# A three-layer interaction network on one core: the spread of the hidden half at its own relu, in two lays, and layer 1's weights on the x queue

## What is computed

```python
h = x0
for i in range(3):
    Wk = Ws[i].reshape(128, H, 32)            # H = 32, then 64, 64
    xk = relu(einsum('bhd,bmd,ohm->bod', h, x0, Wk) + b[i][None, :, None])
    if i != 2:
        outs.append(xk[:, :64]); h = xk[:, 64:]
    else:
        outs.append(xk)
return concatenate([o.sum(axis=-1) for o in outs], axis=1)      # (512, 256)
```

## Time and profile before

| | us |
|---|---|
| three runs | 1838.84, 1838.84, 1838.52 (median 1838.84) |
| the profiled execution, its own time | 1838.24 |
| its span | 1836.4 |
| PE busy | 1799.4 |
| DVE busy | 1555.1 |
| POOL busy | 1464.3 |
| ACT busy | 1096.3 |

### The profile page before, as it was taken

The page is one execution under the profiler, slowest core; times in us unless marked ns, Lnnn a source line. Parts: engine busy times, 40 slices in busy tenths (PEclk is TensorE's granted clock), DMA queues, the critical chain, the costliest instruction groups (busy, mean ns, idle before and its releaser), DMA issues.

```text
span 1836.4 us, 17679 instructions
## 1 busy us (share of the span) xinstructions
PE 1799.4 (98%) x6284; PEld 1184.2 (64%) x6284; DVE 1555.1 (85%) x851; ACT 1096.3 (60%) x899; POOL 1464.3 (80%) x323
## 2 busy tenths in 40 slices
PE   4899999999999999999999999999999999999998
PEld 2566666666666666666666666666666666666665
DVE  5989888888888888898888888888888988888886
ACT  3665666656566656656666565666566566665663
POOL 2787887877877878878878778778788788787785
PEclk9999999999999999999999999999999999999999
DMA  6333323323323333333233233233332332332310
GB/s 230 130 96 119 129 85 129 130 80 128 130 84 129 114 101 129 95 121 129 85 129 131 80 128 121 93 129 114 101 129 87 129 129 85 129 131 79 129 33 20
DMA packets 56455, 205.78 MB, mean 112 GB/s; under 512 B 12721, under 2 KB 14001, under 8 KB 47921
## 3 DMA queue, kind: packets, MB, share of 16 engines
q1 hardware_dynamic: 55408, 204.00, 33.3%
q10 hardware_dynamic: 960, 0.66, 0.1%
HBM read 153.75 MB, written 0.52 MB: 84 GB/s over the span
## 4 chain that ended last, share of the span: by engine, by line
PE 93%; issue 1%; DVE 1%; ACT 1%; POOL 0%; POOLq 0%; SPq 0%; DMA 0%; ACTq 0%
PE ACC L440 23%; PE ACC L456 19%; PE ACC L453 19%; PE ACC L450 19%; PE ACC L431 11%; PE ACC L434 3%; DVE ZS L257 1%; POOL ZL L339 0%; ACT ZH L361 0%; POOLq L71 0%; DVE ZW L252 0%; ACT HP L354 0%; DMA H<-H 0%; SPq L168 0%; DVE S L278 0%
## 5 line engine op out<-in xcount | busy, mean ns | idle before, releaser
L339 POOL TENSOR_TENSOR ZL<-ZS,ZH 128x2048 fp32r<-128x2048 f32 x319 | 1464.1, 4617 | 366.5 <-ACT ZH L361 366.5
L361 ACT ACTIVATE ZH<-ZS 128x2048 fp32r<-128x2048 f32 x384 | 734.6, 1913 | 599.7 <-PE ACC L456 415.3
L257 DVE TENSOR_TENSOR ZS<-HP,X 128x2048 f32<-128x2048 f32 x384 | 870.7, 2281 | 149.0 <-ACT HP L354 149.0
L450 PE MATMUL ACC<-ZH,WL 128*128 128x512 f32 x1536 | 498.3, 446 | 8.0 <-ACT ZH L361 8.0
L440 PE MATMUL ACC<-ZW,WF 128*128 128x512 f32 x1024 | 460.2, 592 | 0.0
L456 PE MATMUL ACC<-ZL,WH 128*128 128x512 f32 x1536 | 421.5, 396 | 8.2 <-POOL ZL L339 8.0
L453 PE MATMUL ACC<-ZH,WH 128*128 128x512 f32 x1536 | 421.6, 396 | 0.0
L450 PEld LDWEIGHTS ACC<-ZH,WL 128*128 128x128 f32 x1536 | 289.9, 189 | 153.3 <-issue 99.6
L252 DVE TENSOR_TENSOR ZW<-HP,X 128x2048 f32<-128x2048 f32 x128 | 292.3, 2283 | 101.2 <-PE ACC L440 101.2
L456 PEld LDWEIGHTS ACC<-ZL,WH 128*128 128x128 f32 x1536 | 287.6, 188 | 81.4 <-POOL ZL L339 11.5
L453 PEld LDWEIGHTS ACC<-ZH,WH 128*128 128x128 f32 x1536 | 289.4, 188 | 70.6
(11 more groups left out here) (32 smaller groups left out, 165.5 us busy)
## 6 DMA issues: line engine op xcount, KB each, us to landing
X<-in_xrows SPq DMA_DIRECT2D x62, 2048.0 KB, 7.6
H<-H SPq DMA_DIRECT2D x512, 64.0 KB, 2.0
XD<-in_xdup SPq DMA_DIRECT2D x64, 256.0 KB, 3.0
H<-H SPq DMA_DIRECT2D x128, 128.0 KB, 2.3
X<-in_xrows SPq DMA_DIRECT2D x4, 1024.0 KB, 9.8
X<-in_w SPq DMA_DIRECT2D x6, 256.0 KB, 13.1
WF<-in_w SPq DMA_DIRECT2D x2, 256.0 KB, 12.8
out<-XD SPq DMA_DIRECT2D x3, 128.0 KB, 1.8
```

The costliest lines, as they stand in the source:

```text
L257: nc.vector.tensor_tensor(ZS[:, n % SSLOTS, :, :], h, x, ALU.mult).then_inc(prod_ready, 1)
L339: nc.gpsimd.tensor_tensor(ZL[:, n % SSLOTS, :, :], ZS[:, n % SSLOTS, :, :], ZH[:, n % SSLOTS, :, :], ALU.subtract).then_inc(low_by_pool, 1)
L361: nc.scalar.activation(ZH[:, n % SSLOTS, :, :], ZS[:, n % SSLOTS, :, :], ACT.Copy).then_inc(high_ready, 1)
L450: nc.tensor.matmul(ACC[layer][:, :], wl[:, g, :], ZH[:, n % SSLOTS, g, :], start=(k == 0 and g == 0), stop=False)
```

## The change

Three things. The relu of the hidden half has a semaphore of its own, `hidden_done`, and SP issues the spread on that. The spread is one DMA for lay 0 and three for lay 1 (64, 32 and 32 rows), all from the relu's rows, with a semaphore for each lay; ACT copies each lay to PSUM when it has landed, and DVE waits for the first copy ahead of product 0 and for the second ahead of product 2. The loads of `W1` and `W1T` move from ACT's queue to SP's behind the first half of x of tile 0, bias and identity behind the second half.

```diff
             def spread_hidden(t, layer):
-                sp.wait_ge(relu_done[layer], t + 1)
+                sp.wait_ge(hidden_done[layer], t + 1)
                 lay0, lay1 = H[layer][:, 0, :], H[layer][:, 1, :]
                 src = HID if layer == 0 else 0
-                sp.dma_start(lay0[HID - src:2 * HID - src, :], lay0[src:src + HID, :]).then_inc(h_loaded[layer], 16)
-                for p in range(0, 128, BLK):
-                    half = src + (BLK if p % HID == 0 else 0)
-                    sp.dma_start(lay1[p:p + BLK, :], lay0[half:half + BLK, :]).then_inc(h_loaded[layer], 16)
+                rows = lay0[src:src + HID, :]
+                sp.dma_start(lay0[HID - src:2 * HID - src, :], rows).then_inc(lay0_loaded[layer], 16)
+                sp.dma_start(lay1[BLK:BLK + HID, :], rows).then_inc(lay1_loaded[layer], 16)
+                sp.dma_start(lay1[0:BLK, :], rows[BLK:HID, :]).then_inc(lay1_loaded[layer], 16)
+                sp.dma_start(lay1[128 - BLK:128, :], rows[0:BLK, :]).then_inc(lay1_loaded[layer], 16)
 
             load_xd(0)
             load_x_half(0, 0)
+            sp.dma_start(W1[:, :, :], w1).then_inc(w1_loaded, 16)
+            sp.dma_start(W1T, w1t).then_inc(w1t_loaded, 16)
             load_x_half(0, 1)
+            sp.dma_start(bias_sb[:, :], bias).then_inc(small_loaded, 16)
+            sp.dma_start(ident[:, :], ident_in).then_inc(small_loaded, 16)
...
             def product(i, layer, q):
                 t = i - layer
-                if q == 0:
-                    dve.wait_ge(h_copied[layer - 1], t + 1)
+                if q % 2 == 0:
+                    dve.wait_ge(h_copied[layer - 1], 2 * t + 1 + q // 2)
...
             def copy_hidden(t, layer):
-                act.wait_ge(h_loaded[layer], 16 * (1 + NB) * (t + 1))
+                act.wait_ge(lay0_loaded[layer], 16 * (t + 1))
                 if t >= 1:
                     act.wait_ge(prod_ready, split_before(t + layer, layer + 1, NS - 1) + 1)
-                nc.scalar.activation(HP[layer][:, :, :], H[layer][:, :, :], ACT.Copy).then_inc(h_copied[layer], 1)
+                nc.scalar.activation(HP[layer][:, 0, :], H[layer][:, 0, :], ACT.Copy).then_inc(h_copied[layer], 1)
+                act.wait_ge(lay1_loaded[layer], 48 * (t + 1))
+                nc.scalar.activation(HP[layer][:, 1, :], H[layer][:, 1, :], ACT.Copy).then_inc(h_copied[layer], 1)
...
                 if t >= 1:
-                    act.wait_ge(h_copied[layer], t)
-                nc.scalar.activation(H[layer][hid, 0, :], ACC[layer][hid, :], ACT.Relu, bias=b[hid, :])
+                    act.wait_ge(h_copied[layer], 2 * t)
+                nc.scalar.activation(H[layer][hid, 0, :], ACC[layer][hid, :], ACT.Relu,
+                                     bias=b[hid, :]).then_inc(hidden_done[layer], 1)
...
-            act.dma_start(W1[:, :, :], w1).then_inc(w1_loaded, 16)
-            act.dma_start(W1T, w1t).then_inc(w1t_loaded, 16)
-            act.dma_start(bias_sb[:, :], bias).then_inc(small_loaded, 16)
-            act.dma_start(ident[:, :], ident_in).then_inc(small_loaded, 16)
```

More of the change, by code:

```diff
@@ L119, in cin_kernel @@
         xd_copied = sem("xd_copied")
-        h_loaded = [sem("h_loaded2"), sem("h_loaded3")]
+        lay0_loaded = [sem("lay0_loaded2"), sem("lay0_loaded3")]
+        lay1_loaded = [sem("lay1_loaded2"), sem("lay1_loaded3")]
+        hidden_done = [sem("hidden_done2"), sem("hidden_done3")]
         h_copied = [sem("h_copied2"), sem("h_copied3")]
```

## The result

The changed kernel took 1833.46 us (median of 7 runs, 1832.48 to 1834.18) against 1838.84 us before: a ratio of 0.9971 (95% interval 0.9959 to 0.9982), 5.4 us less. I had said 1832.1, in a range of 1829.2 to 1834.8. The execution that was profiled took 1833.86.

The account below looks back on a forecast made before the run. PE (TensorE) was taken to bound the kernel, leaving only its idle time at start and end. 4.8 + 1.7 + 0.25 = 6.75 us off 1838.24 gave 1831.5, plus 0.6 for the median 1832.1 us; range 1829.2 to 1834.8.

Parts of the forecast that it names:

- The bound and the place: PE sets the pace between 65.80 and 1780.00 us, so gains lie in the start and a little in the end.
- the 0.35 that I took: Steady state: some 0.35 us more ACT copying per tile, hidden by ACT's waits for PE, so zero cost.
- The first matmul: Start: with layer 1's weights on SP's queue, the first matmul comes 4.95 us earlier than 14.73.
- The spread of tile 0: Start: issued at 16.85 instead of 22.5, held behind the loads on its queue, landing at 22.6 and 23.3.
- the term of 4.8 us: Tile 0: PE restarts for layer 2 at 27.65 instead of 32.42, 4.8 us won.
- Its split: Of tile 0's 4.8 us, about 3.3 from the earlier spread alone and 1.5 from the moved loads.
- Tile 1's 1.7 us: Tile 1: its spread meets no backlog, so the weights' rounding and PE's restart come 1.7 us sooner.
- The end's 0.25: Last tile: the second rounding no longer waits 0.28 us for its product, so the end comes 0.25 us sooner.
- Sum: Whole kernel: 6.75 us off, span 1836.4 to 1829.65, median 1832.1 us.
- Rival (a): Start: the loads don't hold the spread, which lands at 19.15; gain 10.15 us, 1828.7; 10%.
- Rival (b): Start: loads and spread 1 to 2.5 us slower on one queue, or second lay trails; 1833.1 to 1834.6; 17%.
- the forecast's own 1830.8 to 1833.0: Whole kernel: the times for the forecast case itself, a gain of 5.8 to 8 us, given 61%.

Follow-up runs that it names:

- the spread alone: The changed kernel with layer 1's weights, bias and identity back on ACT's queue, timed twice: 1834.39 and 1834.29 us.
- the loads alone: The kernel before with only the four loads (W1, W1T, bias, identity) moved to SP's x queue: 1836.39 us, ratio 0.9987.
- the later weights: The changed kernel with layer 3's weights (1 MB) loaded behind tile 0's spread: 1829.68 us; two versions with further reordering: 1827.63 and 1827.21 us.
- the second execution: The changed kernel itself, unaltered, timed and traced again in another job: 1832.46 us, ratio 0.9964 to the kernel before.
- the last kernel: The changed kernel with layer 3's weights and layer 2's plain weights loaded behind tile 0's spread, and weights rounded before ACT's copies: 1827.21 us.
- the third execution: The changed kernel itself, unaltered, timed and traced a third time: 1832.70 us, ratio 0.9967 to the kernel before.
- the four executions: Three of the changed kernel (1833.46, 1832.46, 1832.70 us) and one of it with ACT's copies doubled for tiles 3 to 59 (1832.73 us).

## Why the prediction was right, and where it was not

**The bound and the place.** Right. PE has no idle time between 60 and 1775 us, and none in the middle with 2.3 us more on ACT in a round either. The change adds 0.2 us in a round (11.1 over 62), and not the 0.35 that I took from the start's rows: by the medians a copy of one lay takes 0.584 us and one of both 1.012, which makes 0.31, and successive records overlap in the busy time. The 0.3 us for each activation that I took from the Trainium skill stands there for one whose bias is an operand, and these copies have none: 512 columns more cost 0.43 us, which leaves 0.16 us beside the columns.

**The first matmul.** 9.75 forecast, 8.96 measured, since x landed at 6.1 (1.19 + 4.9) and not 6.8: W1 beside it had cost more than 0.6 us. It made no difference, as what follows waits for the queue.

**The spread of tile 0.** The mechanism was as said: issued about 6 us sooner, then held by the loads on its queue. The size was off. "Its first DMA lands at 22.6, the three for the other lay at 23.3" became 24.6 and 25.8 in the first profile, 22.9 and 23.7 in the second, 24.3 and 25.3 in the third. Two things failed in it. One is the end of the loads: I let them land at 22.3, as before, and the last landed at 23.6, 22.6 and 23.5 (9.33 + 14.3 for the first). That is up to 1.3 us, and it lies in the last one or two of sixteen parts, the middle ones being there at 22.0, 21.7 and 21.9. The other is the rate: I let the spread's 384 KB pass at 390 GB/s, 1.0 us; the rate row shows 164 to 307 while most of them pass, which is about 1.7 us for 384 KB. PE's restart, 27.65 in the forecast, was at 29.79, 27.91 and 29.33. So the term of 4.8 us measured 2.6, 4.5 and 3.1.

**Its split.** 3.3 for the spread and 1.5 for the loads. In one job, the loads added 1.6 to the spread alone. The 3.3 was too much: I had worked it out by the first lay and the product, and left out that the second lay lands at 25.9 and ACT's roundings stand behind its copy. PE's restart with the spread alone is 2.5 and 1.4 us sooner than before (29.89 and 30.98), the latter with slower first matmuls. That the loads' gain mostly goes into waiting is shown by the run with the loads alone: 5.0 us at the issue became 1.65 at the restart. That bytes ahead on the queue are what it waits for is shown by the later weights.

**Tile 1's 1.7 us.** From its relu to PE's restart: 55.48 - 41.06 = 14.42 before, 51.42 - 38.69 = 12.73 after, and 49.27 - 36.55 = 12.72 in the second execution. 1.7, to the tenth, and PE kept 0.81 and 0.52 us of idle where I had 0.5. From restart to restart it is 1.4 in the first execution and 1.7 in the second (23.06 before, 21.63 and 21.36 after). In the first, where the second lay trailed by 1.2 us and not 0.8, tile 1's relu came 8.90 us behind PE's first restart and not 8.64.

**The end's 0.25.** From PE's second restart to the span's end: 1780.92 before, 1780.68 after. 0.24, but that is luck, for it isn't gained where I said. From the relu of 1812.74 (1808.35 after) to the end it is 23.66 us before and 23.75 after, 23.63 in the other two executions: next to nothing. The second rounding does end sooner, 4.29 us behind that relu instead of 4.76, but DVE's low part behind it takes 4.94 us and not 4.55 and ends at 9.33 against 9.42. What was gained lies 20 us ahead of it. Before, PE's matmuls of a low part started 1.22 us behind the group ahead of them (1792.23, 1793.45), just after GpSimd had ended that low part at 1793.39; after, 0.94 us behind (1788.22, 1789.16), the low part being ready at 1788.96. With the next group that makes 0.39 us, and about as much (0.37 and 0.38) in the other two executions.

**Sum.** For the profiled execution 1829.65 of span was forecast and 1832.1 measured; of the 2.45 us, 2.1 are there at PE's first restart, and 0.3 more at its second. The medians came within 1.4, 0.4 and 0.6 us. Rival (a), a spread not held by the loads, didn't come about in the change; the last kernel is what it would look like. Rival (b) describes the first and the third execution (restarts at 29.79 and 29.33, in its 28.7 to 30.2), and the median of the result, 1833.46, lies in its 1833.1 to 1834.6 and not in the forecast's own 1830.8 to 1833.0, where the two later medians lie. The second execution (27.91) is the forecast's.

**What stays open.** What makes one or two of a DMA's sixteen parts fall behind the others, by up to 1.7 us, and whether an early issue has a hand in it: in the four executions the earlier the issue, the later the last part, but four are too few to say. And why PE's first eight matmuls take 5.4 us in one execution and 6.8 in another.

## What to carry to other kernels

A load that is moved to bring the first matmul forward pays only as far as the next transfer on the path gets through; look at what its queue still carries when it is issued, and put loads that are needed late behind it. For a small transfer on the path the order in one queue was the safer tool here: what stood behind it landed over 5 us after it, whereas on a second queue it shared the engines with what the first still carried. A DMA is there only with the last of its sixteen parts, so a forecast from bytes and rate gave the middle part here, and the last was up to 2 us later. And one trace of a kernel whose start is bound by transfers is one draw: the part that was re-timed beside the whole gave the answer, the two traces side by side the wrong one.

## What the hardware showed that I had not expected

The spread's copies from SBUF to SBUF (rows of 2 KB) went at no more than 262 GB/s alone, and 0.39 MB, most of it theirs, in 1.7 us (229 GB/s) behind the loads, with the DMA engines at nine tenths of their time or more, where loads went at 287 to 471, 389 on average, in the 1.5 us just before. Of the sixteen parts of a DMA behind a backlog the last came 0.5 to 2.0 us after the middle one. A transfer of 64 KB on ACT's queue took 11.0 us beside 2 MB on SP's, and 2.0 us alone. And PE's idle time before a restart understated what could be won there by 0.57 us (0.54 shown, 1.11 won), since it is counted from the modelled end of matmuls that the next would have overlapped.
